# First layer's experts: from all eight on every token to the best two through slots in DRAM

## The reference, cut to what matters

```
flat = hn.reshape(b * s, d)                       # 4096 x 128
probs = softmax(flat @ Wr); topv, topi = top_k(probs, 2)
topv = topv / sum(topv)
w = sum(one_hot(topi, 8) * topv[..., None], axis=1)
g = einsum('td,edf->etf', flat, Wg)               # 8 experts, f = 256
u = einsum('td,edf->etf', flat, Wu)
o = einsum('etf,efd->etd', silu(g) * u, Wd)
out = clip(residual + einsum('te,etd->td', w, o), -100, 100)
x = x + gb * out
```

## Time and profile before

| | |
|---|---|
| median of 3 runs | 1832.56 us (1827.0 to 1834.64) |
| the profiled execution's own time | 1822.73 us |
| its span | 1820.9 us, granted clock 0.912 |
| busy: PE, DVE, ACT, POOL | 1512.4, 1012.6, 695.9, 392.1 us |
| DMA | 38.61 MB, mean 21 GB/s |
| c0 / c1 / first mixture | 25 to 350 / 350 to 858 / 858 to 1163 us |
| handover / c2 / second mixture | 1163 to 1213 / 1213 to 1650 / 1650 to 1821 us |

### The profile page before, as it was taken

How to read it: one execution, slowest core, us unless ns; L and a number is a source line. 1 busy time by engine, 2 the same in 40 slices (tenths; PEclk the granted TensorE clock), 3 DMA queues, 4 the chain that set the end, 5 groups by cost and what they waited for, 6 DMA issues and landing times.

```text
span 1820.9 us, 32157 instructions
## 1 busy us (share of the span) xinstructions
PE 1512.4 (83%) x10612; PEld 1076.2 (59%) x10612; DVE 1012.6 (56%) x2534; ACT 695.9 (38%) x1533; POOL 392.1 (22%) x616
## 2 busy tenths in 40 slices
PE   4899999689989989997899999688888888883580
PEld 2677777466666666665788888554444444441450
DVE  2555555354545555554788888556656666553103
ACT  1344444324444535445222222125545455452230
POOL 1222222132213222210000000121313223215206
PEclk9899999879999999998999999859989899896795
DMA  8100000100000000000000000200000000100233
GB/s 257 31 6 3 4 3 6 36 6 4 7 6 7 6 7 1 1 1 1 1 1 1 0 0 1 64 0 6 10 6 9 5 10 9 28 1 30 87 93 92
DMA packets 37276, 38.61 MB, mean 21 GB/s; under 512 B 4688, under 2 KB 30448, under 8 KB 36752
## 3 DMA queue, kind: packets, MB, share of 16 engines
q1 hardware_dynamic: 35088, 32.73, 6.1%
q0 software_dynamic: 2048, 4.20, 0.8%
HBM read 28.46 MB, written 8.45 MB: 20 GB/s over the span
## 4 chain that ended last, share of the span: by engine, by line
PE 65%; DVE 12%; POOL 9%; issue 8%; ACT 3%; DMA 1%; DVEq 1%; SPq 0%; POOLq 0%; ACTq 0%
PE ps_out L1889 10%; PE ps_four L1028 7%; PE ps_max L1039 6%; PE ps_max L1809 5%; PE ps_work L1746 4%; DVE row_max L1621 4%; PE ps_four L1835 3%; PE ps_four L1721 2%; PE ps_max L1799 2%; PE ps_four L1799 2%; PE ps_four L1726 2%; PE ps_four L1746 2%; PE ps_max L1095 2%; PE ps_four L1086 2%; POOL rstd L1237 2%
## 5 line engine op out<-in xcount | busy, mean ns | idle before, releaser
L1621 DVE TENSOR_REDUCE row_max<-ps_max 128x3 f32<-128x384 f32 (+1 forms) x640 | 370.3, 603 | 138.8 <-PE ps_max L1809 129.4
L1460 ACT ACTIVATE attn_f<-ps_four 128x384 f32<-128x384 f32 (+1 forms) x640 | 329.6, 532 | 230.2 <-PE ps_four L1835 229.0
L1809 PE MATMUL ps_max<-k_st,q_st 24*128 24x256 f32 (+2 forms) x1280 | 269.0, 346 | 52.4 <-DVE row_max L1621 47.2
L1889 PE MATMUL ps_out<-attn_f,v_all 128*9 128x256 f32 (+3 forms) x2560 | 309.6, 366 | 0.9 <-ACT attn_f L1450 0.8
L1809 PEld LDWEIGHTS ps_max<-k_st,q_st 128*128 128x128 f32 (+1 forms) x1280 | 180.5, 204 | 112.2 <-DVE row_max L1621 54.6
L1835 PE MATMUL ps_four<-q_st,k_st 26*128 26x256 f32 (+2 forms) x1280 | 240.9, 324 | 0.2 <-ACT attn_f L1460 0.2
L1889 PEld LDWEIGHTS ps_out<-attn_f,v_all 128*9 128x9 f32 (+1 forms) x2560 | 100.5, 93 | 132.7 <-issue 29.7
L1835 PEld LDWEIGHTS ps_four<-q_st,k_st 128*128 128x128 f32 (+1 forms) x1280 | 170.7, 200 | 3.9 <-ACT attn_f L1460 2.0
L1039 PEld LDWEIGHTS ps_max<-wd,o_both 128*128 128x128 f32 x1024 | 134.8, 193 | 18.5 <-DVE o_both L930 7.6
L1799 PE MATMUL ps_max<-masks,ident_bf 128*128 128x256 bf16 (+1 forms) x384 | 118.6, 309 | 29.5 <-DVE row_max L1621 20.3
L1039 PE MATMUL ps_max<-wd,o_both 128*128 128x128 f32 x1024 | 136.7, 277 | 5.5 <-DVE o_both L930 5.5
(11 more groups left out here) (238 smaller groups left out, 2490.1 us busy)
## 6 DMA issues: line engine op xcount, KB each, us to landing
wd<-in_L_ffn_W SPq DMA_DIRECT2D x16, 256.0 KB, 2.8
gates_all<-in_select SPq DMA_DIRECT2D x3, 1024.0 KB, 7.1
mod<-mod_dram SPq DMA_DIRECT2D x16, 192.0 KB, 3.0
x_all<-in_L_attn_x SPq DMA_DIRECT2D x8, 256.0 KB, 6.2
slots_dram<-attn_f SPq DMA_DIRECT2D x8, 256.0 KB, 5.4
mod<-mod_dram SPq DMA_DIRECT2D x16, 128.0 KB, 2.9
gates_all<-mod_dram SPq DMA_DIRECT2D x2, 1024.0 KB, 9.2
h_tok<-slots_dram SPq DMA_DIRECT2D x8, 256.0 KB, 2.9
```

The costliest lines, as they stand in the source:

```text
L1460: nc.scalar.activation(probs[:, h % 4, 0:w], ps_exp[:, h % 3, 0:w], ACT.Exp, scale=c.scale).then_inc(exp_done, 1)
L1621: nc.vector.tensor_reduce(row_max[:, r2, 0:blocks, h], src, AX_X, ALU.max).then_inc(max_done, 1)
L1809: ins = nc.tensor.matmul(bank[:, at:at + keys.stop], q_st[rows, r, g, k * P:(k + 1) * P], k_st[rows, r, c.k_group(h), keys], start=not c.c ...
L1889: last = nc.tensor.matmul(ps_out[base:base + c.hd + 1, at + first:at + S], v_tok[c.index][:, r, kb, h // (c.heads // c.kv), :], probs[:, h ...
```

## The change

The first mixture is computed for the two best experts of a token only. An expert owns a region of 4096 rows in a new tensor `slots0_dram` (36864 rows of 512 bytes, zeroed by 72 transfers of 256 KB in c0's segments). A token's row is scattered twice, to the next free row of either expert. `TURNS` now has three turns for this layer: batches 0 to 11 (routed in segments 13 and 14 of c1), 12 and 13 (segment 15), 14 and 15 (after c1). `dve_pair_rank` and `pe_pair_rank` find the places, and `dve_tiles` lists the 72 tiles of 128 rows and their experts. The tiles are computed two to a step, in 36 steps, in fp32: rows loaded by SP, turned by PE, up product of 512 columns (gate and up of one expert), tanh, two DVE products, turned again, down product, stored to `y0_dram`. The expert number and row offset are read from `tile_ids` into registers (`value_load`). In c2, POOL gathers two rows for every token (`gather_pair`) and DVE adds them (`combine`). The splitting of the weights and of the tokens, `accumulate` and `pool_moe` go. `select` of c2 is loaded ahead of the mixture.

```diff
-        TURNS = ((0, 0, NB * BLK, NB), (1, 0, SOON, NB + NB - 2), (1, SOON, NB * BLK, 2 * NB))
+        TURNS = ((0, 0, 24, 12), (0, 24, SOON, NB - 2), (0, SOON, NB * BLK, NB),
+                 (1, 0, SOON, NB + NB - 2), (1, SOON, NB * BLK, 2 * NB))
+        FIRST_ROUTES = {"best": ((13, 2), (15, 2)), "exp": ((13, 3), (15, 3)), "first": ((13, 4), (15, 4)),
+                        "second": ((13, 7), (15, 6)), "rank_mm": ((13, 15), (15, 8)), "rank": ((14, 0), (15, 10))}
...
+        def sp_moe(sp):
+            def load(s):
+                for t in range(2):
+                    row = sp.value_load(tile_ids[0:1, 0, 2 * s + t:2 * s + t + 1], min_val=0, max_val=SLOTS0 - P)
+                    if t == 0:
+                        at_least(sp, slots_mm, s - 3)
+                    sp.dma_start(x_rows[:, s % 4, t, :], slots0_dram[bass.ds(row, P), :]).then_inc(slots_load[s % 4], 16)
...
+        def scatter0(pool, k):
+            for n in range(2):
+                nc.gpsimd.indirect_dma_start(slots0_dram[:], bass.IndirectOffsetOnAxis(ap=pair_put[:, n, k:k + 1], axis=0),
+                                             hn_all[:, k, :], None).then_inc(scattered0, 16)
+        def may_scatter0(pool, turn):
+            pool.wait_ge(routed, turn + 1)
+            pool.wait_ge(rt_kept, TURNS[turn][3])
+        def scatter0_beside(pool, b, h):
+            at = (b - 14) * 16 + h - 2
+            if at == 0:
+                pool.wait_ge(zero_store, 16 * (8 + ZEROED))
+                may_scatter0(pool, 0)
+            if 0 <= at < 24:
+                scatter0(pool, at)
+            if b == 15 and h >= 12:
+                if h == 12:
+                    may_scatter0(pool, 1)
+                scatter0(pool, 24 + h - 12)
+        def gather_pair(pool, b, r):
+            if not isinstance(b, int) or b >= RING:
+                pool.wait_ge(comb_done, b - RING + 1)
+            nc.gpsimd.tensor_copy(get_now[:, r], pair_get[:, :, bass.ds(b * BLK, BLK)]).then_inc(get_copied, 1)
...
+            for n in range(2):
+                for k in range(BLK):
+                    nc.gpsimd.indirect_dma_start(y_pair[:, r, n, k, :], None, y0_dram[:],
+                                                 bass.IndirectOffsetOnAxis(ap=get_now[:, r, n, k:k + 1], axis=0)
+                                                 ).then_inc(pair_load[r], 16)
...
+        def combine(dve, b, r):
...
+            nc.vector.tensor_copy(w_now[:, r2], pair_w[:, :, bass.ds(b * BLK, BLK)]).then_inc(w_copied, 1)
...
+            dve.wait_ge(pair_load[r], 16 * (b - r) + 64)
+            for k in range(BLK):
+                last = nc.vector.scalar_tensor_tensor(y_sum[:, k, :], y_pair[:, r, 0, k, :], w_now[:, r2, 0, k:k + 1],
+                                                      block_of(res_all, b * BLK + k), ALU.mult, ALU.add)
...
+            nc.vector.tensor_scalar(y_sum, y_sum, CLIP, -CLIP, ALU.min, ALU.max).then_inc(comb_clip, 1)
...
+            nc.vector.tensor_tensor(xs, xs, y_sum, ALU.add).then_inc(comb_done, 1)
...
         def pe_moe(pe):
+            def up(s):
+                experts = [pe.value_load(tile_ids[0:1, 1, 2 * s + t:2 * s + t + 1], min_val=0, max_val=E0 - 1)
+                           for t in range(2)]
+                pe.wait_ge(x_t_out, s + 1)
+                at_least(pe, act_done, s - 1)
+                for t in range(2):
+                    last = nc.tensor.matmul(gu_banks[s % 2][:, t, :], x_t[:, s % 2, t * P:(t + 1) * P],
+                                            wgu[:, :, bass.ds(experts[t], 1), :].rearrange("p i o f -> p i (o f)"),
+                                            start=True, stop=True)
...
+            for s in range(STEPS + 2):
+                if s < STEPS:
+                    up(s)
+                if s > 1:
+                    down(s - 2)
+                if s + 2 < STEPS:
+                    turn_rows(s + 2)
+                if 0 < s <= STEPS:
+                    turn_act(s - 1)
...
             def start(c):
+                if c.index == 2:
+                    pool.wait_ge(gets_ready, 1)
+                    for s in range(2):
+                        pool.wait_ge(y_store[s], 16 * (STEPS // 2))
+                    gather_pair(pool, 0, 0)
+                    gather_pair(pool, 1, 1)
...
             def segment(c, b, r):
+                if c.index == 2 and (not isinstance(b, int) or b + 3 < NB):
+                    gather_pair(pool, b + 3, (r + 3) % RING)
...
+                    if c.index == 1 and isinstance(b, int):
+                        scatter0_beside(pool, b, h)
...
+                    if c.index == 2 and h == 0 and flags(b)[1]:
+                        combine(dve, b + 2, (r + 2) % RING)
```

626 lines of the change are left out of this document (374 added, 252 removed).

## The result

The changed kernel takes 1839.97 us (median of 6 runs, 1837.54 to 1840.55); the kernel before, beside it, 1831.59. The ratio is 1.0044, 95% interval 1.003 to 1.0059: about 8 us slower, where 1781 was forecast. By the mark of 9 us that the prediction set, this is no change; what is clear is that the forecast gain of 51 us did not come. The profiled execution's own time is 1840.55 us, its span 1838.6, its granted clock 0.853 (0.912 before).

The account below looks back on a forecast made before the run. PE was taken to bound the first mixture (298.5 of 305 us), PE and DVE alternating in c2. Mixture -88.2, handover +5.3, c2 +32 made -51: span 1770, median 1781, range 1742 to 1850.

Parts of the forecast that it names:

- The mixture: First mixture: first up product at 926, 36 steps, last down product ending at 1074.4 instead of 1162.6; gain 88.2 us.
- T: Mixture, one step of two tiles: 3.6 us of PE work plus 0.3 of register loads sticking out, 3.9 us.
- The rival of exposed loads: Mixture: PE's sequencer stands for each register load, 0.54 us each; T 5.8, time 1849, deciding from T 5.3; chance 0.20.
- The handover: From the mixture's end to c2's start: 16.9 us where it was 11.6, loss 5.3 us.
- The softmax parts: c1's segment 13: some 20 DVE operations, 8 us, half taken as exposed: 4 us ahead of the scatters' start at 822.
- Then 56 x 1.263 = 70.7, two `rstat` pairs in between 2.4, a wait of 2 for turn 1's rank: End of c1: POOL's scatters from 822 delay batch 15's `rstat`; logits at 901.7, 44.5 us later than before.
- The 20 to 30 us that PE was to stand ahead of `rht`: Sign in c1's segment 15: PE idles 20 to 30 us because `rmul` of batch 14 waits behind POOL.
- the rest of the way: Logits to mixture: places after 9.5 us, eight scatters landing by 922.3, load 2.65, transposition and copy 1, first up product 926.
- 32 us for `combine`: c2: `combine` takes 2.7 us of DVE in each of 14 segments, 2.3 each taken as exposed, 32 us.
- POOL's gathers of b+3: c2: 5.6 us of gathers a segment, placed where POOL is idle: 0; uncovered, 5.6 us on 13 segments.
- the `rstd` of my rival: c2: gathers delay the statistics' `rstd`, so POOL becomes the bound, 13 x 5.6 us: 1854; chance 0.07.

Follow-up runs that it names:

- experiment 6: Changed kernel with all 64 scatters behind c1's last step on POOL, none beside c1: 1838.43 us, ratio 1.0075 to the kernel before.
- experiment 12: Changed kernel with a pause of about 1.5 us on POOL after each four of the 56 scatters beside c1: 1827.36 us, ratio 1.0005.
- 1: Kernel before plus only 56 indirect scatters on POOL in c1's segments 14 and 15, nothing of the change: 1880.18 us, ratio 1.0309.
- 2: Kernel before plus 56 indirect gathers from DRAM at the same places of c1, in place of scatters: 1885.89 us, ratio 1.0308.
- 3: Kernel before plus 56 plain POOL operations where the added scatters stood, no transfers added: 1844.66 us, ratio 1.01.
- 4: Kernel before plus 56 plain POOL operations, SP sending a plain transfer of 128 rows after each: 1851.27 us, ratio 1.0136.
- 5: Kernel before plus 56 scatters, with two plain POOL operations (2.6 us forecast) after each four: 1882.88 us, ratio 1.031.
- 14: Changed kernel with early, unrepeated register loads, `combine` in five pieces, and only 28 of 64 scatters beside c1, in paused fours: 1782.33 us, ratio 0.9766.
- 16: As 14 but without the pauses: rows of 8, 12 and 8 scatters beside c1, then 36 behind it: 1803.22 us, ratio 0.9844.
- experiment 9: Changed kernel with `combine`'s arithmetic left out of c2, one tiny operation in its place, gathers kept: 1804.86 us, ratio 0.9885.
- experiment 10: Changed kernel without the gathers of c2's segments (batches 0 to 2 keep theirs), `combine` adding stale rows: 1815.11 us, ratio 0.9927.
- 11: Changed kernel with `combine` of batch b+3 cut into five pieces in slots 8 to 12 of segment b: 1829.63 us, ratio 1.0003.

## Why the prediction was wrong

**The mixture: right in its sum, by luck.** Forecast T 3.9, measured 3.91; 148 us forecast, 147 measured. Two errors cancelled: without the loads a step takes 3.27 us where I had 3.6, and the loads stick out 0.64 where I had 0.3. The rival of exposed loads was right in kind: they are on the path, at 0.16 us each, far from the 0.44 from which it decides. That its 1849 lies near the measured time is chance. The Trainium skill (DMA: Bandwidth & Descriptors, Latency and other measured facts) has about 600 ns for a `tensor_load`; the row here shows 298 ns for the load, and with the register operations behind it one follows the other in 0.64 us; here the measured row counts.

**The handover: near.** 16.9 forecast, 15.2 measured.

**The softmax parts: mis-sized.** I took half of 8 us and let the rank of 24 blocks move only the start of the scatters. In experiment 6 c1 ends 14 us later without a scatter beside it: DVE's routing stands in front of `row_max` and PE. The start of the scatters, 824.7 for 822, nearly fitted, since both parts were in it.

**The step that failed: "Then 56 x 1.263 = 70.7, two `rstat` pairs in between 2.4, a wait of 2 for turn 1's rank".** POOL's pace is right (1.264), but I took it for granted that PE's side goes on meanwhile. It doesn't: while a row of indirect transfers runs without a pause, PE's products are reported up to 24 us late, so ACT and DVE come late with what POOL's `rstat` needs. POOL idles ahead of each of the three `rstat` pairs, in the midst of the row that I took as the bound:

```profile
843.96 0.19 POOL L1460 TENSOR_TENSOR var_eps_rt<-ssq_rt,eps 128x2 f32<-128x2 f32 x1 [4.14 <-ACT attn_f L1597]
...
900.80 0.19 POOL L1460 TENSOR_TENSOR var_eps_rt<-ssq_rt,eps 128x2 f32<-128x2 f32 x1 [15.37 <-ACT attn_f L1597]
...
925.72 0.19 POOL L1460 TENSOR_TENSOR var_eps_rt<-ssq_rt,eps 128x2 f32<-128x2 f32 x1 [8.77 <-ACT attn_f L1597]
```

These 28.3 us, and a start 2.7 us later, less the 2 that I took for turn 1's rank and under 1 elsewhere, put batch 15's logits at 929.9, 28.2 us late of forecast. With pauses between the scatters (experiment 12) no such idle time is left: each `rstat` follows POOL's own work at once, and batch 15's is 9.4 us earlier in spite of 21 us of pauses. The 20 to 30 us that PE was to stand ahead of `rht` are 3.3; PE stands for ACT in their place, 18.2 us at the longest. Experiments 1 to 5 show the cause in the kernel before, 6, 12, 14 and 16 in the changed one. What I said of the rest of the way was near: first scatter of the last turn after 8.6 us (9.5), landing after 11.2 more (11.1), but 7.8 us to the first up product where I had 3.7: SP's first loads with a computed row take 1.05 us each, where four took 0.54 each in the earlier trace rows, and two tiles have to be turned first.

**c2: one term right, one missing.** 32 us for `combine` against 29 by experiment 9. The second step that failed is the 0 for "POOL's gathers of b+3": they cost 21 us by experiment 10. They do so neither through the `rstd` of my rival, for which DVE waits 7.5 us in c2 as against 7.2 before, nor, by the traces of experiments 10 and 11, through waits for late reports: PE's own work takes longer. The busy time of the kernel before, over its c2:

```profile
1174.00:1645.00 471.00, 391.41 (x2882) 223.61 (x2884) 282.11 (x694) 221.32 (x453) 115.49 (x185) 0.87 0.04 10
```

As many matmuls take 411 us in the changed kernel where they took 391, at a mean granted clock of 0.80 where it was 0.87: more of the stretch was at 1.2 GHz in place of 2.4. Without the gathers they take 390, without `combine` 409; what `combine` costs is idle time of PE instead. Why the clock is lower beside gathers stays open: PE idles nearly as long without them (120 us of c2 for 124).

**The end: 6 us that are probably not the change's.** SP's stores of the result drag behind DVE in the changed kernel's profile (16 stores in 43.83 us); the span ends 9.5 us after DVE's last sum, in the profile of before 3.1. All the experiments' profiles have 7.4 to 9.8, those of the kernel before with additions too. So the profile of before looks like the odd one, which may be why its own time lay 9.8 us below its median.

Against the forecast span of 1770: +31.5 to the first up product, -1.6 in the mixture, -1.7 in the handover, +34.0 in c2, +6.4 at the end, 1838.6. Nearly the whole error is in what runs beside the attentions, and nothing of it in the stage that was rewritten. The range held the time (1742 to 1850); the direction did not come out.

**What stays open:** what delays PE's reports. No record of the trace shows a resource that is busy in it: the packets of all indirect transfers take 2.3% of the 16 engines' time. It is not POOL's being busy (3), not the bytes (4), not the direction (2), not the new code (1). It needs a row: fours with pauses of 1.5 to 2 us between them left single reports at most 2.8 us late in c1; rows of eight made them up to 7 us late, one of twelve up to 9 (16). Why fours in c2 made a report 1.8 to 2.0 us late and no longer did when `combine` was cut is open too. One rival was not tested: the recording itself. Every execution here, the timed ones too, has its span and clock from the profiler. Beside indirect transfers the trace lacks some of PE's reports (24 of 896 in c2 of the changed kernel), and in c2 of the kernel before and of experiment 10 it lacks none. Whether a row of indirect transfers costs as much in an execution that is not recorded, no run shows.

## What to carry to other kernels

An indirect transfer can cost more than its 1.26 us on POOL: here a row of them beside matmuls stalled the other engines through PE. So try small groups with a pause between them, and no more ahead of a step that others wait for than fit in POOL's idle time there; this was worth 25 us, 10 by the order and 14 by the pauses. A register load on PE's queue is not free because the array is busy for most of the step: place it right behind queued products, and load a value that is needed twice once. And a new stage is to be costed by what its preparation and its aftermath do to the stages beside it: the mixture's 158 us were all spent there, and three small edits (early loads, `combine` in pieces, fewer scatters beside c1 in groups) brought some 50 of them back (ratio 1.0044 to 0.9766).

## What was unexpected of the hardware

- Reports of PE's products up to 24 us late beside 32 indirect transfers in a row, gathers or scatters alike (23.6, 23.9 and 24.0 us in three programs); none of ACT's, DVE's or POOL's; none beside plain transfers of the same bytes or beside POOL's other work. Pauses of 2 us after each four took over 25 us of POOL's time and cost nothing that the runs show (ratio 1.031 against 1.0309).
- Beside the gathers of c2 PE's matmuls took 399 to 413 us at a granted clock of 0.83 to 0.80 (five traces); without these gathers 390 us at 0.85 (one trace).
- Two powers on a tile of 128x2 (1.5 us) do as a pause.
- A TENSOR_LOAD of one word takes 298 ns on PE's queue, and one follows the other, with its register operations in between, after 0.64 us.
- "Idle for ACT `h_both`, 0.34" was named on a wait that PE's own sequencer ended: where a line computes its address, look at the queue's rows too.
